# The last message-passing layer of a graph network on one core: TensorE fetches 4 and 5 of every 16 source rows instead of 4, and ScalarE's and VectorE's orders are rewritten

## The reference, cut to what matters

```python
def _L1_gnn_ref(x, edge_index, edge_attr, W_edge, b_edge, W1, b1, gamma, beta, W2, b2):
    src, dst = edge_index
    ea = edge_attr @ W_edge.T + b_edge          # 200000 x 16 by 16 x 64
    msg = relu(x[src] + ea)                     # a fetched row for each edge
    agg = segment_sum(msg, dst, num_segments=6250)
    h = (1.0 + GIN_EPS) * x + agg
    h = h @ W1.T + b1
    ...                                         # batch norm over the nodes, relu
    return h @ W2.T + b2
```

## Time and profile before

| | |
|---|---|
| median of 3 runs | 8745.62 us (8744.52 to 8752.81) |
| span of the profiled execution, first to last instruction | 6476.7 us |
| the profiled execution's own device time | not given beside its span |
| TensorE busy, share of the span | 5692.6 us, 88% |
| VectorE busy | 4958.1 us, 77% |
| ScalarE busy | 4658.0 us, 72% |
| GpSimd busy | 4758.4 us, 73% |
| mean granted clock of TensorE, share of full | 0.958 |

### The profile page before, as it was taken

One profiled execution on the slowest core, in us unless ns is written; L12 is line 12 of the kernel. 1 busy time (PEld: TensorE's weight loads), 2 busy tenths in 40 slices (PEclk: granted clock), 3 DMA queues, 4 the chain that ended last, 5 costly groups with the idle time before them and its releaser, 6 DMA issues.

```text
span 6476.7 us, 96630 instructions
## 1 busy us (share of the span) xinstructions
PE 5692.6 (88%) x25094; PEld 4699.3 (73%) x25094; DVE 4958.1 (77%) x7554; ACT 4658.0 (72%) x6121; POOL 4758.4 (73%) x4960
## 2 busy tenths in 40 slices
PE   2699999999679999999949999999968999999996
PEld 1577787777468888888738888888846777777774
DVE  8699999999669999999939999999984344334433
ACT  1588888888468888888828888888854555555553
POOL 3777777777677777777777777777767777777774
PEclk9899999999789999999959999999978999999996
DMA  9577777777345555555525555555544444444441
GB/s 390 193 243 240 240 239 240 241 240 243 117 136 177 181 179 174 178 182 176 172 73 174 177 174 180 182 174 175 181 122 112 142 141 142 136 143 139 144 141 52
DMA packets 453281, 1147.44 MB, mean 177 GB/s; under 512 B 159661, under 2 KB 224799, under 8 KB 417669
## 3 DMA queue, kind: packets, MB, share of 16 engines
q1 hardware_dynamic: 279472, 919.26, 39.5%
q0 software_dynamic: 159376, 175.97, 15.2%
q10 hardware_dynamic: 14404, 51.92, 2.0%
HBM read 750.45 MB, written 396.27 MB: 177 GB/s over the span
## 4 chain that ended last, share of the span: by engine, by line
POOL 38%; issue 25%; DVE 19%; ACT 13%; PE 1%; DMA 1%; ACTq 1%; DVEq 1%; POOLq 0%; SPq 0%
POOL sb_xl L516 33%; DVE pG L1158 6%; DVE sb_s_run L1200 5%; ACT sb_turn_out L719 5%; ACT sb_hot L719 4%; ACT sb_v_in L719 3%; POOL sb_hot_f L516 3%; POOL marks L520 2%; DVE sb_s L1441 2%; ACT pB L719 1%; DVE sb_e_in L1223 1%; DVE sb_lr L1221 1%; DVE sb_s L1219 1%; DVE sb_mark L1104 1%; PE pG L604 1%
## 5 line engine op out<-in xcount | busy, mean ns | idle before, releaser
L604 PE MATMUL pG<-sb_xl_parts,sb_hot 128*128 128x476 f32 (+1 forms) x24010 | 5312.2, 379 | 424.4 <-ACT sb_xl L719 312.0
L604 PEld LDWEIGHTS pG<-sb_xl_parts,sb_hot 128*128 128x128 f32 x24010 | 4486.7, 189 | 1292.4 <-issue 695.9
L516 POOL DMA_INDIRECT sb_xl<-xl_table,sb_idx x4557 | 4363.5, 958 | 1400.6 <-issue 1391.2
L1158 DVE COPY_PREDICATED pG<-sb_pick_turn,pG 128x408 f32<-128x408 int32 (+7 forms) x2352 | 1071.7, 457 | 940.0 <-ACT sb_pick_turn L719 808.0
L719 ACT ACTIVATE sb_hot<-sb_wide 128x1792 fp32r<-128x1792 bf16 (+1 forms) x784 | 1427.5, 1834 | 103.9 <-ACT sb_turn_out L719 67.7
L1200 DVE TENSOR_TENSOR_SCAN sb_s_run<-pB,sb_v_in 128x272 f32<-128x272 f32 (+3 forms) x1470 | 1094.9, 772 | 4.1 <-ACT sb_turn_out L719 4.0
L719 ACT ACTIVATE sb_turn_out<-sb_s_run 128x1088 f32<-128x1088 f32 (+3 forms) x395 | 834.7, 2113 | 11.4 <-DVE sb_s_run L1200 11.1
L719 ACT ACTIVATE sb_xl<-pG 128x136 f32<-128x136 f32 (+4 forms) x826 | 248.1, 303 | 612.9 <-DVE pG L1158 506.0
L1197 DVE TENSOR_TENSOR_SCAN pB<-sb_same_c,pB 128x1024 f32<-128x1024 f32 x294 | 671.7, 2285 | 0.1
L719 ACT ACTIVATE pB<-sb_mark 128x960 f32<-128x960 f32 x294 | 563.8, 1918 | 80.2 <-DMA sb_mark<-marks 62.5
L719 ACT ACTIVATE sb_v_in<-sb_v_g 128x1024 f32<-128x1024 f32 x291 | 601.1, 2065 | 0.0
(11 more groups left out here) (237 smaller groups left out, 2357.2 us busy)
## 6 DMA issues: line engine op xcount, KB each, us to landing
state_rows<-sb_turn_out SPq DMA_DIRECT2D x294, 576.0 KB, 3.4
sb_wide<-hots SPq DMA_DIRECT2D x147, 1120.0 KB
sb_mark<-marks SPq DMA_DIRECT2D x294, 512.0 KB
sb_wide<-hots SPq DMA_DIRECT2D x147, 896.0 KB
sb_xl<-xl_table,sb_idx POOLq DMA_INDIRECT x4557
sb_wide<-codes SPq DMA_DIRECT2D x49, 1120.0 KB
hots<-sb_wide SPq DMA_DIRECT2D x49, 1120.0 KB
marks<-sb_hot_f SPq DMA_DIRECT2D x32, 1568.0 KB
```

What stands on the lines that cost most here:

```text
L516: return pool.indirect_dma_start(out=dst, out_offset=None, in_=table, in_offset=bass.IndirectOffsetOnAxis(ap=index, axis=0))
L604: product = pe.matmul(pG[:, bank + a - lo, 0:GB * n], hot[k][:, m, a * P:(a + 1) * P], rows[:, :, 0:n], start=(m == 0 and part == 0), stop ...
L1158: return dve.copy_predicated(rows[:, :, 0:n], over(pick_turn[:, k, stage, lo:hi], n), rows[:, :, at:at + n])
```

## The change

The linear stage takes the attention layers' division: TensorE makes 4 blocks of a turn k = 0 and 5 of a turn k = 1, GpSimd fetches 12 and 11. The product of the attributes goes in two row halves: four matmuls with 64 rows and 256 columns in place of two with 128 rows and 512 columns, the upper and the lower rows into different PSUM banks, and the host lays the attributes out to match. It now stands between TensorE's two shares. ScalarE does the ReLU of the turn before first, then widens, and writes the masks one turn ahead; VectorE takes the sums of the turn before ahead of the selection. TensorE's wait for its own first share is gone, in all four layers.

```diff
-LINEAR = 4
-LIN_SHARES = tuple(((n - LINEAR, n - 2), (n - 2, n)) for n in FETCHED)
-LIN_SHARE_BANK = (0, 2)
-LGD = G - LINEAR
...
 # sync
-                    sp.wait_ge(s_xl[k], (i + 1) * (16 * LGD) + LAYERS * PAIRS * 16 * GD[k])
+                    sp.wait_ge(s_xl[k], (i + (LAYERS * PAIRS + 1)) * (16 * GD[k]))
 # gpsimd
-                    turn_gathers(i + LAYERS * PAIRS, k, range(LGD))
+                    turn_gathers(i + LAYERS * PAIRS, k, range(GD[k]))
 # tensor, pe_gather
                 pe.wait_ge(s_rows[q], copied)
                 pe.sem_inc(s_passed, 1)
-                if q:
-                    pe.wait_ge(s_pg[q - 1], copied + 1)
-                    pe.sem_inc(s_passed, 1)
 # tensor, linear stage
-                    for q in range(2):
-                        pe.wait_ge(s_wide[q], 2 * i + (LAYERS * TURNS + k + 1))
-                        pe.sem_inc(s_passed, 1)
-                        pe_gather(2 * i + (LAYERS * TURNS + k), q, k, C)
+                    pe.wait_ge(s_wide[0], 2 * i + (LAYERS * TURNS + k + 1))
+                    pe.sem_inc(s_passed, 1)
+                    pe_gather(2 * i + (LAYERS * TURNS + k), 0, k, C)
                     pe.wait_ge(s_attr[k], (i + 1) * 16)
                     pe.wait_ge(s_ea_used, 2 * i + k)
                     pe.sem_inc(s_passed, 1)
                     for q in range(2):
-                        product = pe.matmul(pE[:, q * 512:(q + 1) * 512], attr[:, k, q * P:(q + 1) * P], w_blk[:, :],
-                                        start=True, stop=True)
+                        for half in range(2):
+                            rows = slice(half * 64, half * 64 + 64)
+                            product = pe.matmul(pE[:, half * 512 + q * 256:half * 512 + q * 256 + 256], attr[rows, k, q * P:(q + 1) * P],
+                                                w_blk[rows, half * 256:half * 256 + 256], start=True, stop=True)
                     product.then_inc(s_ea[k], 1)
+                    pe.wait_ge(s_wide[1], 2 * i + (LAYERS * TURNS + k + 1))
+                    pe.sem_inc(s_passed, 1)
+                    pe_gather(2 * i + (LAYERS * TURNS + k), 1, k, C)
 # scalar, linear_turn
-                act.wait_ge(s_sel[0], turn_all)
-                act.wait_ge(s_sel[1], turn_all)
-                turn_masks(i, k)
-                rows_copied(turn_all + 1, use, 0, k, C)
-                rows_copied(turn_all + 1, use, 1, k, C)
-                ...   # the two small copies and the ReLU of this turn
-                if not first:
-                    hand_out_linear(turn_all, (use + k - 1) * 16, turn - 1, 1 - k)
-                if not last:
-                    widen_both(s_hot_in, i * 16 + ((LAYERS - 1) * PAIRS + 2) * 16, turn_all + 1, k, C)
+                if not first:
+                    relu_rows(turn - 1, turn_all - 1)
+                    if not last:
+                        widen_both(s_hot_in, (i + k) * 16 + ((LAYERS - 1) * PAIRS + 1) * 16, turn_all, 1 - k, C)
+                rows_copied(turn_all + 1, use, 0, k, C)
+                if not last:
+                    turn_masks(i + k, 1 - k)
+                if not first:
+                    hand_out_linear(turn_all, (use + k - 1) * 16, turn - 1, 1 - k)
+                rows_copied(turn_all + 1, use, 1, k, C)
 # vector, linear_turn
-                select_rows(turn_all + 1, turn_all + 1, selects, k, 0, C)
-                select_rows(turn_all + 1, turn_all + 1, selects + 1, k, 1, C)
                 if not first:
                     dve.wait_ge(s_lin_relu, turn)
                     dve.wait_ge(s_same, turn_all)
                     linear_sums(2 * i + (LAYERS * TURNS + k - 1))
+                select_rows(turn_all + 1, turn_all + 1, selects, k, 0, C)
+                select_rows(turn_all + 1, turn_all + 1, selects + 1, k, 1, C)
 # host
-    attr_t = attr.reshape(P, TURNS, 2, 8, KE).transpose(1, 3, 4, 2, 0).reshape(TURNS, P, 2 * P)
+    attr_t = attr.reshape(P, TURNS, 2, 2, 4, KE).transpose(1, 2, 4, 5, 3, 0).reshape(TURNS, P, 2 * P)
```

More of the change, by code:

```diff
@@ L566, in _, with share @@
                     gather(node_rows[:, b, 0:C], agg_rows, last_edge[:, b:b + 1]).then_inc(s_nrow[g], 16)
-        def share(k, q, n=TW):
-            shares, banks = (LIN_SHARES, LIN_SHARE_BANK) if n == C else (SHARES, SHARE_BANK)
-            lo, hi = shares[k][q]
-            return lo, hi, banks[q]
+        def share(k, q):
+            lo, hi = SHARES[k][q]
+            return lo, hi, SHARE_BANK[q]
         def place(psum, i):
@@ L736, in rows_copied @@
                 act.wait_ge(s_used[k], used)
-                lo, hi, bank = share(k, q, n)
+                lo, hi, bank = share(k, q)
                 copy(xl[:, k, GD[k] + lo:GD[k] + hi, 0:n], pG[:, bank:bank + hi - lo, 0:n]).then_inc(s_rows[q], 1)
@@ L931, in _, with relu_rows @@
             low_part(GROUPS - 1)
-            def linear_turn(i, k, first=False, last=False):
-                use = i + LAYERS * PAIRS
-                turn = 2 * i + k
-                turn_all = 2 * i + (k + LAYERS * TURNS)
-                act.wait_ge(s_sel[0], turn_all)
-                act.wait_ge(s_sel[1], turn_all)
-                turn_masks(i, k)
-                rows_copied(turn_all + 1, use, 0, k, C)
-                rows_copied(turn_all + 1, use, 1, k, C)
+            def relu_rows(turn, turn_all):
                 act.wait_ge(s_sums, turn_all)
@@ L946, in linear_turn @@
                 act.activation(v_lin[:, :, 1:G1], s[:].rearrange("p g c -> p c g"), ACT.Relu).then_inc(s_lin_relu, 1)
+            def linear_turn(i, k, first=False, last=False):
+                use = i + LAYERS * PAIRS
+                turn = 2 * i + k
+                turn_all = 2 * i + (k + LAYERS * TURNS)
+                if not first:
[5 more added lines that the diff above has]
+                    turn_masks(i + k, 1 - k)
                 if not first:
                     hand_out_linear(turn_all, (use + k - 1) * 16, turn - 1, 1 - k)
-                if not last:
-                    widen_both(s_hot_in, i * 16 + ((LAYERS - 1) * PAIRS + 2) * 16, turn_all + 1, k, C)
+                rows_copied(turn_all + 1, use, 1, k, C)
+            turn_masks(0, 0)
             widen_both(s_hot_in, (LAYERS - 1) * (PAIRS * 16) + 16, LAYERS * TURNS, 0, C)
@@ L960, in _ @@
                     linear_turn(i, k)
-            for k in range(2):
-                linear_turn(PAIRS - 1, k, last=True)
+            linear_turn(PAIRS - 1, 0)
+            linear_turn(PAIRS - 1, 1, last=True)
+            relu_rows(TURNS - 1, (LAYERS + 1) * TURNS - 1)
             hand_out_linear((LAYERS + 1) * TURNS, (LAYERS + 1) * (16 * PAIRS) - 16, TURNS - 1, 1)
@@ L1153, in select_stage @@
             def select_stage(k, q, stage, width=TW):
-                lo, hi, bank = share(k, q, width)
+                lo, hi, bank = share(k, q)
                 n = (3, 2, 1)[stage] * width
```

4 lines of the change are left out of this document (2 added, 2 removed).

## The result

The changed kernel took 9003.52 us (8971.9 to 9038.19, 4 runs) where the kernel before, measured beside it, took 8745.07 (8736.06 to 8752.81, 4 runs): a ratio of 1.0297 [1.0276, 1.0318], 3% slower, where 0.8% faster was forecast.

What follows compares the result with a forecast made beforehand. GpSimd's gathers, with a closed VectorE-ScalarE loop on the same 15 us a turn, were taken to bound the linear stage; -63.3, -5.4 and -2.0 sum to -70.7, so 8745.6 becomes 8674.9 us, range 8650 to 8735.

Steps and rivals of the forecast that it cites:

- Sum: Whole kernel: span falls 70.7 us to 6406.0; 2268.9 us of the median lie outside it, untouched, giving 8674.9.
- The wait for itself in the attention layers: Layers 0 to 2: removing TensorE's 0.5 us wait per turn changes nothing; taken as 0, at most 39 us.
- Gathers: Linear stage: 1127 gathers instead of 1176 at 1.250 us, first to last start 1407.9 us: -63.3 us.
- End of the stage: Linear stage's end: last s 2.6 us after the last gather starts, -5.4 us; hand-out already done, -2.0 us.
- The loop: Linear stage: with masks a turn ahead, ScalarE needs 9.8 to 10.6 us, VectorE 7.2; neither bounds.
- What is queued behind what: Linear stage: ScalarE waits up to 3.6 us for the one-hot load; it fits behind the gathers, cost taken as 0.
- The product in halves: Linear stage, TensorE: the row halves overlap enough that GpSimd stays the bound; E between 0.86 and 2.70 us, taken as 1.3.
- E: TensorE time the new product adds to a linear-stage turn; taken as 1.3 us, GpSimd-bound up to 1.62.
- the second rival: Linear stage: row changes stall TensorE, up to 8783 us; chance 0.07 for E 2.14 to 2.49, 0.07 above.
- The clock: TensorE's granted clock stays at 1.00 of full in a fuller linear stage; effect 0.
- The rivals: TensorE-bound serial halves, 8687; row-change stalls, to 8783; loop not really opened, 8735 to 8765, chance 0.06; stretched time, 8650, 0.07.
- The whole time stretches with the span: Whole kernel: unprofiled runs take 1.35 times the span everywhere, so the gain is 95 us: 8650; chance 0.07.

Runs made afterwards that it cites:

- d_before: The kernel before, unchanged, profiled in the slow condition: 8743.4 us, with the kernel before at 8746.79 in its set.
- b_nowait: The kernel before without TensorE's wait for its own first share, quick condition: 6479.65 us, ratio 1.0004 to the kernel before.
- c_same: The changed kernel, unchanged, run again in the quick condition: 6411.84 us, ratio 0.9894 to the kernel before.
- e_nowait: The kernel before without TensorE's wait for its own first share, slow condition: 8830.68 us, ratio 0.9924 to the kernel before.
- the sixth set: Slow-condition runs measured together: kernel before 8905.6 us, changed kernel with TensorE's wait put back 8736.98, e_nowait 8830.68.
- a_lin4: The changed kernel with the earlier division, 4 blocks in every linear-stage turn, all else kept, quick condition: 6466.93 us, ratio 0.9985 to the kernel before.

## Why the prediction was wrong

**"Sum", the step that failed first.** It took 2268.9 us of the median to lie outside the span, where nothing in the change could touch them. They lay inside: the span of d_before is 8741.6 of 8743.4 us. Nothing spoke for putting them outside except that the profile showed nothing of them. The profile and the runs came from different conditions, and the difference is spread over all four stages as stretches of slow issue. Everything in the forecast was worked out for a program without them.

**"The wait for itself in the attention layers", the step that decided the sign.** "I take 0" is right in the quick condition: b_nowait is within 0.1%, and layers 0 to 2 of c_same keep their length to 0.9 us. In the condition that was timed, taking the wait out makes layer 0 longer by 183.7 (e_nowait against d_before) to 188.6 us, and putting it back takes 183.2 off again (2088.7 - 1905.5). The reason given, that TensorE's gap is not in the chain of layer 0, holds for the quick condition alone: in the slow one VectorE's selections there wait for 471 us even with the wait, and 649 without. With layers 1 and 2 the attention layers give back 341.9 us against 105.2 gained in the linear stage. That the removed wait is the cause has five traces of layer 0 for it, one execution each, and is argued for no more than a part of layers 1 and 2; the totals of the sixth set do not bear it out for the kernel before.

**"Gathers", "End of the stage", "The loop".** Right in the sum, measured in the quick condition: the first to last `s` fell by 1461.2 - 1394.7 = 66.5 us, the gathers took 1409.0 against 1407.9 forecast, and the whole time fell by 69.6 against 70.7. The last `s` starts 6295.4 - 6292.2 = 3.2 us after the last gather, not 2.6. That fewer gathers alone would gain nothing, because the closed loop lies on the same 15 us, is not shown: the orders alone gain 10 us (a_lin4), and the split alone was not run.

**"What is queued behind what".** Right: ScalarE waits 2.5 us a turn for the one-hot matrix, at most 3.3 where up to 3.6 was allowed, and the turn stays at 14.38 us, so it costs nothing.

**"The product in halves".** Right in kind and near in size: E was taken as 1.3, below the limit of 1.62. Measured are 1.06 us from the product's first weight load to the next fetching one. E as the prediction uses it, from the start of the last fetching matmul before the product to the first one after it less one step of 0.20, is 1.36 - 0.20 = 1.15 us in c_same. Four pairs at 0.216 would be 0.86. The other 0.29 us are what the two changes of rows can have cost: 0.09 before the first pair (0.29 after the last fetching matmul, where 0.20 is the step), 0.10 between the first two, 0.09 behind the last (0.31, where 0.22 is the step). The Trainium skill, "TensorE: Matmul & The Clock Gate", part 3 on packing small matmuls, says that matmuls on different row groups run at the same time; these rows agree. By the Trainium skill, "TensorEngine Tiling (Array Packing)", Key Properties, a change of tiling mode drains TensorE; here the two changes of a turn cost at most 0.29 us together, on pairs that run side by side, and E stays below the limit of 1.62, so the second rival did not come about.

**"The clock".** Right in the quick condition (granted 1.00 over the linear stage of c_same). In the slow one the mean over the span falls to 0.83, behind the stretches.

**The rivals.** None was the case. "The whole time stretches with the span" saw that the extra 2269 us might lie in all stages, but made one factor of it: by 1.35 each stage would have kept its share. In fact the linear stage of the kernel before stretched 2179.4 / 1461.2 = 1.49 fold, layer 0 1.32 fold, and what a single wait does to that stretching no factor could tell.

**What stays open.** Why the sequencers issue an instruction only every 0.7 us in those stretches, and why every second or third turn. A fetch of instructions by DMA is not to be seen in the changed kernel's profile, and what GpSimd's gathers have to do with it was not tested. Why a set is in one condition or the other: all three sets of four kernels were quick, and the four sets of one or two kernels (the first measurement among them) slow, on the same chip 12 both ways, but a connection through which the number could act is not known. Why the removed wait moves the stretches in the turn and lengthens those of layer 0, and why its removal shortens the linear stage of the kernel before. Why the kernel before took 160 to 170 us more in the sixth set.

## What to carry to other kernels

Before a profile is used for a forecast, compare its span with the time of the runs. When they differ by 35%, the profile explains how the program works but not the time that is to be forecast, and the forecast should say what it would be if the missing time lay inside, spread over every stage. Compare versions only within one set of runs, and put a part from which nothing is forecast, as here a wait taken out of three layers, apart from the one that is to bring the gain, so that each can be kept or left alone.

## What the runs showed that was not expected

- One program has two levels of time that differ by 35%, 6477 and 8740 us, both steady to 0.4% within a set for the kernel before, and the unprofiled runs can be on one and the profile on the other.
- In the slow level TensorE's and SyncE's sequencers go down to an instruction every 0.7 us or a multiple of it for some 8 to 20 us at a time, every second or third turn and at the same place in it, while GpSimd's gathers keep their step of 1.24 us.
- A third fewer matmuls on TensorE, with 13 gathers a turn in their place, made the changed kernel 10% slower there, and the linear stage no faster.
- The stretches come without an instruction packet in the DMA queues, and as much with the loops written out as with them.
- A wait of 0.5 us a turn on TensorE, free in the quick level, goes with some 185 us of layer 0 in the slow one, while its removal takes 109 us off the linear stage of the kernel before.
- fp32 matmuls on the lower and the upper 64 rows run side by side: eight passes of 256 columns in 1.06 us, and the two changes between 128 and 64 rows around them cost 0.29 us at most together.
